# A graph kernel's message pass: one gather per tile of edges instead of one per slot, into a ring of 64 tiles

## What is computed

```python
em = jnp.concatenate([x[src], x[dst]], axis=-1)
em = jax.nn.relu(layer_norm(em @ msg_w + msg_b, msg_g, msg_beta))
em = em * edge_weights[:, None]
msgs = jax.ops.segment_sum(em, dst, num_segments=num_nodes)
```

## Time and profile before

| | us |
|---|---|
| median of 3 runs | 8210.3 (8195.7 to 8234.3) |
| span of the profiled execution | 6732.1 |
| median less that span | 1478.2 |
| first to last gather of the message pass | 4579.7 to 6590.8 |

### The profile page before, as it was taken

The page is one execution under the profiler, slowest core; times in us unless marked ns, Lnnn a source line. Parts: engine busy times, 40 slices in busy tenths (PEclk is TensorE's granted clock), DMA queues, the critical chain, the costliest instruction groups (busy, mean ns, idle before and its releaser), DMA issues. The chain is left out here.

```text
span 6732.1 us, 124645 instructions
## 1 busy us (share of the span) xinstructions
PE 5109.7 (76%) x33726; PEld 4567.4 (68%) x33726; DVE 4555.6 (68%) x15714; ACT 2981.2 (44%) x10333; POOL 4624.6 (69%) x4875
## 2 busy tenths in 40 slices
PE   5788887888887378888888888866676677776775
PEld 4666676676766268777777777856666666666664
DVE  5777777777777746666666665676666666666667
ACT  3444444444444322222222222255666666666666
POOL 4777777777775077777777777706777777777771
PEclk7788888888888656666666676679999999999997
DMA  8544444444443322222222222222222222222221
GB/s 173 151 116 115 115 112 114 115 115 115 114 114 85 103 61 63 64 62 63 63 63 62 64 62 63 62 86 60 54 54 53 54 54 54 54 54 54 54 54 29
DMA packets 334708, 534.90 MB, mean 79 GB/s; under 512 B 105502, under 2 KB 222767, under 8 KB 333665
## 3 DMA queue, kind: packets, MB, share of 16 engines
q0 software_dynamic: 181264, 439.20, 25.7%
q1 hardware_dynamic: 143462, 83.65, 4.6%
q10 hardware_dynamic: 9323, 4.08, 0.3%
HBM read 489.59 MB, written 42.61 MB: 79 GB/s over the span
## 5 line engine op out<-in xcount | busy, mean ns | idle before, releaser
L932 POOL DMA_INDIRECT arena<-rows,slot_src x3222 | 3079.0, 956 | 1027.3 <-issue 930.8
L722 POOL DMA_INDIRECT arena<-msg_rows,slot_src x1611 | 1521.4, 944 | 523.7 <-issue 483.9
L1130 ACT ACTIVATE arena<-psum 128x512 f32<-128x512 bf16 x808 | 480.2, 594 | 1552.3 <-PE psum L978 1528.4
L2034 PE MATMUL psum<-arena 128*128 x3232 | 704.9, 302 | 500.4 <-DMA arena<-msg_rows,slot_src 447.3
L1019 PE MATMUL psum<-arena 128*128 128x145 f32 x3232 | 978.6, 394 | 0.0
L1268 DVE TENSOR_TENSOR arena<-arena,psum 128x290 f32 x1616 | 731.2, 452 | 292.8 <-DVE arena L1268 176.6
L2034 PEld LDWEIGHTS psum<-arena 128*128 128x128 f32 x3232 | 524.6, 204 | 567.6 <-issue 567.4
L1021 PE MATMUL psum<-arena 128*128 128x145 f32 x3232 | 870.1, 360 | 0.0
L2041 ACT ACTIVATE arena<-psum 128x128 bf16<-128x128 f32 x1616 | 424.1, 277 | 754.5 <-PE psum L2036 754.4
L1205 DVE TENSOR_TENSOR arena<-arena,psum 128x512 f32<-128x512 f32 x808 | 553.6, 685 | 262.5 <-PE psum L1021 255.9
L1034 PE MATMUL psum<-arena 128*128 x3232 | 595.9, 326 | 155.9 <-ACT arena L1130 67.3
(11 more groups left out here) (360 smaller groups left out, 9590.5 us busy)
## 6 DMA issues: line engine op xcount, KB each, us to landing
arena<-rows,slot_src POOLq DMA_INDIRECT x3222
arena<-msg_rows,slot_src POOLq DMA_INDIRECT x1611
arena<-slot_keys SPq DMA_DIRECT2D x100, 128.0 KB
edge_alpha<-arena SPq DMA_DIRECT2D x50, 128.0 KB
arena<-edge_alpha SPq DMA_DIRECT2D x50, 128.0 KB
slot_keys<-lane_keys SPq DMA_DIRECT2D x24, 256.0 KB
arena<-rows SPq DMA_DIRECT2D x6, 1024.0 KB, 10.0
rows<-arena SPq DMA_DIRECT2D x4, 822.0 KB
```

Of the source, the lines that this page charges most:

```text
L722: pool.indirect_dma_start(out=self.buffer[:, v % U, j, :], out_offset=None, in_=self.source, in_offset=bass.IndirectOffsetOnAxis(ap=K.SRC[ ...
L932: pool.indirect_dma_start(out=E.rowbuf[:, r, j, :], out_offset=None, in_=E.source, in_offset=bass.IndirectOffsetOnAxis(ap=K.SRC[:, at:at + ...
L1130: act.activation(E.onehotT[:, v % 2, :, :], E.psT, ACT.Copy).then_inc(E.turned, 1)
L2034: pe.matmul(psH[b][:, j, :], onehotT[:, b, j, :], K.by_dst[:, bass.ds(blocks(v, j), 1), :].rearrange("p b w -> p (b w)"), start=True, stop ...
```

## The change

A tile is gathered once. Tile t goes to place t mod 64 of a ring (`RING = 64`), and both slots of a tile that has two read the same place. The gathers are in tile order, so 1563 instead of 1611 are issued. For this the sources must be there by tile: `tile_sources`, new, runs between `attend` and `second_rows`; it loads `src` from DRAM, turns it with PE and stores it as `tile_sources` in DRAM. `node_loads` loads that over `K.SRC` after the second pass has used it. POOL before each gather waits for the visit that last used the place, and for the tile 24 before to have landed (each of 24 semaphores is used by one tile in flight). SP waits for each tile in order and counts one semaphore, `landed`, up. PE waits for `landed` to reach a value that it works out from a block number in a register, and finds the ring place of each slot from a register as well.

```diff
+def message_rows_in(K, source, ring, summed, landed):
+    pool = K.pool
+    for t in range(TILES):
+        last = t - RING + NB - 1
+        if last >= 0:
+            summed.wait(pool, 0, last // G)
+        at_least(pool, landed, t - ROWS_MOST + 1)
+        pool.indirect_dma_start(out=ring[:, t % RING, :], out_offset=None, in_=source,
+                                in_offset=bass.IndirectOffsetOnAxis(ap=K.SRC[:, t:t + 1], axis=0)
+                                ).then_inc(K.arrived[t % ROWS_MOST], 16)
+def message_rows_landed(K, before, landed):
+    sp = K.sp
+    for t in range(TILES):
+        r = t % ROWS_MOST
+        sp.wait_ge(K.arrived[r], before[r] + 16 * (t // ROWS_MOST + 1))
+        sp.sem_inc(landed, 1)
+def tiles_needed(v, block):
+    last = v * G + G - 1
+    return TILES if last >= USED else (last + 1 - block) & 2047
+def tile_place(slot, block):
+    return (slot + RING - block) & (RING - 1)
@@ second_pass
     rstd, mean = attend(K, D)
+    tile_sources(K, D)
     second_rows(K, rstd, mean)
+def tile_sources(K, D):
...
+    converted.done(pool.memset(given_i[:, full // P:SC, :], 0))
+    converted.after(sp)
+    load(sp, moved, given_i[:, 0:full // P, :], D["src"][0:full // P * P * P].rearrange("(c p e) -> p c e", p=P, e=P))
+    load(sp, moved, given_i[0:full % P, full // P, :], D["src"][full // P * P * P:full * P].rearrange("(p e) -> p e", e=P))
...
+    moved.after(pool)
+    converted.done(pool.tensor_copy(given, given_i))
+    converted.after(pe)
+    for half, cs in enumerate((range(0, 8), range(8, SC))):
+        if half:
+            out.after(pe)
+        for c in cs:
+            last = pe.transpose(K.ps[:, 6 + c % 8 // 4, c % 4 * P:c % 4 * P + P], given[:, c, :], K.ident[:, :])
+        flipped.done(last)
+        flipped.after(act)
+        for a in range(cs[0], cs[-1] + 1, 4):
+            n = min(4, cs[-1] + 1 - a)
+            out.done(act.activation(turned[:, a * P:(a + n) * P], K.ps[:, 6 + a % 8 // 4, 0:n * P], ACT.Copy))
+    out.after(sp)
+    load(sp, moved, K.tile_src, turned)
+    moved.after(sp, pool, K.dve, act)
@@ node_loads
         load(sp, S.late[k], S.h1_T[:, a * P:z * P], K.h1_T[:, a * P:z * P])
+    load(sp, S.tiles_in, K.SRC[:, 0:TILES], K.tile_src[:, 0:TILES])
@@ message_pass
+    S.tiles_in.after(pool)
+    pool.wait_ge(S.q_out, len(CHUNKS))
+    message_rows_in(K, K.prow, ring, summed, landed)
+    message_rows_landed(K, arrived_before, landed)
@@ sums
-        gather.emit(i, v)
         ones.out.wait(pe, i, v)
         scaled.wait(pe, i, v - U)
-        gather.arrived.wait(pe, i, v)
+        pe.wait_ge(landed, tiles_needed(v, blocks(v, G - 1)))
...
-            last = pe.matmul(psH[b][:, j, :], K.ident[:, :], rowbuf[:, b, j, :], start=False, stop=True)
+            last = pe.matmul(psH[b][:, j, :], K.ident[:, :],
+                             ring[:, bass.ds(tile_place(v * G + j, blocks(v, j)), 1), :].rearrange("p b w -> p (b w)"),
+                             start=False, stop=True)
```

More of the change, by code:

```diff
@@ L54 @@
 LOADS = [(b, min(b + 4 * CHUNK, NB)) for b in range(0, NB, 4 * CHUNK)]
+RING = 64
 BIG = 1e30
@@ L1590, in attend @@
     return rstd, minus_mean
+TILES_AT = 2 * REGION + (NB + 1) * AW + 2650
+def tile_sources(K, D):
+    pool, pe, act, sp = K.pool, K.pe, K.act, K.sp
+    SW, full = SC * P, E // P
+    given_i, given = K.arena[:, TILES_AT:TILES_AT + SW].bitcast(i32), K.arena[:, TILES_AT + SW:TILES_AT + 2 * SW]
+    given_i, given = (x.rearrange("p (c e) -> p c e", e=P) for x in (given_i, given))
+    turned = K.arena[:, TILES_AT + 2 * SW:TILES_AT + 3 * SW].bitcast(i32)
+    assert TILES_AT + 3 * SW <= ARENA - 1568
+    K.tile_src = K.dram("tile_sources", [P, SW], i32)
+    moved, converted, flipped, out = (K.dmas("tile_sources_moved"), K.relay("tile_sources_converted"),
+                                      K.relay("tile_sources_turned"), K.relay("tile_sources_out"))
+    converted.done(pool.memset(given_i[:, full // P:SC, :], 0))
+    converted.after(sp)
+    load(sp, moved, given_i[:, 0:full // P, :], D["src"][0:full // P * P * P].rearrange("(c p e) -> p c e", p=P, e=P))
+    load(sp, moved, given_i[0:full % P, full // P, :], D["src"][full // P * P * P:full * P].rearrange("(p e) -> p e", e=P))
+    if full * P < E:
+        load(sp, moved, given_i[full % P:full % P + 1, full // P, 0:E - full * P], row_of(D["src"][full * P:E]))
+    moved.after(pool)
[14 more added lines that the diff above has]
+    moved.after(sp, pool, K.dve, act)
 def second_rows(K, rstd, minus_mean):
@@ L1700, in __init__ @@
         self.late = [K.dmas(f"nodes2_late_in{k}") for k in range(len(LOADS))]
+        self.tiles_in = K.dmas("nodes2_tile_sources_in")
 def node_loads(S, D):
@@ L1987, in message_pass @@
     K.acc = table(K.RF, MW)
-    (rowbuf,) = pieces(K.RA, 0, (F, None))
-    onehotW, junk = pieces(K.RA, NB * F, (P, None), (F, bf16))
+    ring = K.RA[:, 0:RING * F].rearrange("p (t w) -> p t w", w=F)
+    onehotW, junk = pieces(K.RA, RING * F, (P, None), (F, bf16))
     onehot, onehotT, rhs = pieces(K.RL, NB * F, (P, bf16), (P, None), (MW, None))
@@ L2002, in message_pass @@
         Event(K, "message_" + x) for x in ("summed", "squared", "rooted", "inverted", "scaled", "ready", "scattered"))
-    gather = Gather(K, "message", K.prow, rowbuf, [summed])
+    landed, arrived_before = K.sem("message_tiles_landed"), list(K.arrived_before)
     ones = OneHots(K, "message", onehot, onehotT, psT, summed, onehotW, scattered)
@@ L2077, in message_pass @@
     for v in (0, 1):
-        sums(0, v, lambda _, j: blocks_pe(v, j))
+        sums(0, v, blocks_pe)
     scales(0, 0, lambda j: None)
@@ L2092, in message_pass @@
             if at + 2 < VISITS:
-                sums(i, v + 2, lambda _, j: blocks_pe(at + 2, j))
+                sums(0, at + 2, blocks_pe)
             ready.wait(pe, i, v)
```

## The result

| | median of the runs | range | span of the profiled execution | its time |
|---|---|---|---|---|
| before, beside the changed kernel | 8221.67 us | 8195.68 to 8234.33 (4) | 6732.1 us | - |
| changed | 8149.23 us | 8134.46 to 8165.84 (4) | 8132.7 us | 8134.46 us |

The ratio is 0.9914, with 0.9895 to 0.9933 as its 95% interval: 0.9% faster, 72 us on these medians. The forecast was 8172 us and -39 us.

A forecast was written before the change was run, and what follows sets the result against it. It took POOL's gathers to bound the message pass. Terms -60.0 + 20.7 + 0.2 + 0.5 = -38.6 us gave a span of 6693.5, plus 1478.2 around it 8172 us (-0.47%); range 8130 to 8240.

The forecast's parts named there:

- What bounds the kernel: Message pass: POOL's gathers, 1.249 us from start to start, set the pace; a visit of four slots costs 4.99 us.
- a rival of 0.10: Time outside the profile: the 1478 us are the same work running slower, so everything scales, 8163 us; chance 0.10.
- The loop's own pace: Message pass: the loop of PE, ACT and DVE takes 4.38 us a visit, below the gathers' new 4.83.
- 48 gathers fewer: Message pass: 48 gathers at 1.249 us each are saved and count in full, -60.0 us.
- PE's registers: Message pass, PE: five more register expressions a visit, 0.23 us, mostly beside matmuls and covered by the gathers; cost 0.
- The bound of a number load: PE's wait on a register's value: at most a load of eight numbers, 1.2 us; taken at the low end.
- the rival of 8567: PE's wait on `landed`: at 1.2 us extra a visit the loop becomes the bound, 336 us more; chance 0.07.
- Waits on POOL and counting by SP: Message pass: POOL's extra waits hide behind the gather before, 0; SP's hop from landing to PE costs 0.2 us once.
- The sources by tile: Between `attend` and `second_rows`: a chain of load, cast, transposes, copies and store, all counted, 20.7 us (bounds 14 and 36).
- Time around the span: Outside the profiled span: 1478.2 us, the median less the span, taken as unchanged.
- slower throughout: Whole kernel: timed work runs 1.22 times slower than profiled, scaling the gain to -47 us, 8163 us; chance 0.10.
- the rival of 8250: Around the span: the surrounding time grows with some 6600 added instructions, 5.3%, +78 us; chance 0.08.

The follow-up runs named there:

- e3: The changed kernel, unedited, timed and profiled against the kernel before on one chip; ratio 0.9949, span 8277.7 us.
- e2: The kernel before, unedited, profiled again on the same chip as the changed kernel; median 8318.76 us, span 8319.5 us.
- e7: Changed kernel with three of four message-pass gathers left out after the first 64; 1777.7 us from first to last scatter.
- e11: Changed kernel with TensorE's ring places and landed wait as constants instead of register values; 2496.7 us from first to last scatter.
- e6: Changed kernel with 49 more gathers in the message pass, into columns nobody reads; 2482.0 us from first to last scatter.
- e4: Kernel before with only the ring of 64 and SyncE's count, one gather per slot, constants on PE, no sources' stretch; ratio to before 1.0021.
- e5: Kernel before with only the sources' stretch added between attend and second_rows, its result unused; ratio to before 1.0038.
- e8: Changed kernel with three of four gathers after the first 64 replaced by memsets of about 0.95 us; 1779.7 us from first to last scatter.
- e10: Changed kernel with the sources' work laid beside attend, transposes behind loop_edges' product; ratio to before 0.9918, 2415.2 us from first to last scatter.

## Why the prediction was right or wrong

The time came out inside the range and on the side that was forecast, but this was in good part luck: the mechanism behind the forecast was not that of the timed runs, and errors in its terms cancelled. By stages e3 against e2 is -77 in the loop, +14 at its start, +12 for the sources and +10 elsewhere, where the forecast had -60, 0, +21 and +1.

**What bounds the kernel: right for the rows shown, wrong for the runs that are timed.** The step that failed is the first, "so the gathers set the pace". At the timed pace POOL is idle for 0.30 us in each of three gaps and for about 1.35 in the fourth, and PE hardly waits for rows (3.9 us in e2, 8.2 in e3). Yet the gathers do set the length of a visit, by a way that the rows ahead of the prediction don't contain: four gathers, then the pause in which PE's signals come through. The hint was in the table: 1478 us between span and median. I priced it as a rival of 0.10 and should have asked first whether the profile was of the runs at all. The loop's own pace, 4.38 us a visit in the prediction, was near: 4.41 in e7.

**48 gathers fewer, -60.0.** From first gather to last scatter the message pass of e3 is 2480.0 us and that of e2 2543.3: -63.3. The size is right by a coincidence of three terms: from first to last gather -116.9, of it 48 x 1.25 = 60 the gathers and 57 what POOL's pauses lost beyond their 0.30; and +53.6 from the last gather to the last scatter (26.3 to 79.9), since at the end POOL runs further ahead and the last visits are done without gathers. By e11 the 60 alone would not have come. With the registers in place, e6 prices a gather at 67 / 49 = 1.37 us, not 1.249.

**PE's registers, 0.** Wrong in kind. They cost 14 us at the start and, with the waits of POOL as they are in this kernel, are a condition of the gain. The 46 ns of the earlier trace rows hold for the one step a slot of before, also in e2 and e11 (1616 of 1616). Of the 9286 steps of e3, 73 took over 0.1 us, mostly 0.7 and at most 1.4, and none of them after the last gather; in e7, with a quarter of the gathers, it is 13, all at the start. The bound of a number load for the wait on a register, and with it the rival of 8567, is refuted.

**Waits on POOL and counting by SP, 0 and 0.2.** Right: the gap inside a group stays 0.30, and "SPq" ended 11.5 us of POOL's idle time in all. e4, which has both, took 6 us more than e2 in the loop, and that comes from its start.

**The sources by tile, 20.7.** The timeline of the changed kernel:

```profile
2861.46 0.46 DVE L1608 RECIPROCAL arena<-arena 128x49 f32<-128x49 f32 x1 [1.37 <-ACT arena L1607]
2861.95 1.43 SPq L184 DMA_DIRECT2D arena<-in_src  x3
2867.18 1.57 POOL L1637 CAST arena<-arena 128x1664 f32<-128x1664 int32 x1 [67.02 <-DMA arena<-in_src]
...
2868.90 1.94 PE L1643 MATMUL psum<-ident,arena 128*128 128x128 f32 x8 [66.55 <-POOL arena L1637]
...
2874.17 0.35 SPq L184 DMA_DIRECT2D tile_sources<-arena  x1
2877.68 2.65 DVE L1672 TENSOR_SCALAR arena<-arena 128x128 f32<-128x128 f32 x10 [15.76 <-DMA tile_sources<-arena]
```

15.8 us. The chain is as predicted and each term a little too dear: load 5.2 (6.0), cast 1.6 (2.3), transposes and copies 5.3 (5.7), store with its hand-over 3.5 (6.0). The formula of the Trainium skill, DMA: Bandwidth & Descriptors (Anatomy of one DMA), which I had weighed and put aside, is stated for transfers that GpSimd issues, and these are SyncE's; as an estimate it gives 3.95 us for the store, nearer to the 3.5 than my row, and 3.8 for the load, where 5.2 were measured. The time between the passes grew by less than DVE's 15.8 us of waiting: 12 us in e3 and in e5. e5, which has the same stretch, was timed at +0.38% (21 to 42 us by its interval), and its span is 22 us longer, of which 6 lie in the loop of the message pass that it leaves as it was; where the rest comes from stays open.

**Time around the span.** The rival "slower throughout" was the true case, and its 8163 the nearest of all the numbers. But it scaled a sum whose parts don't scale: a gather takes 0.94 us at either pace. The time around the span is 1.8 us and did not grow with 10767 instructions more (I had counted 6600), which ends the rival of 8250.

**What is open.** Why one profiled execution of fourteen ran without the hold: it has 1611 gathers 1.249 us apart without a pause, so gathers are needed for the hold but are not enough. What in the chip holds TensorE, and whether it is the issuing or the transfer of the rows. Why the changed kernel's gain was 0.9% in one comparison and 0.5% in the other, where the kernel before took 8222 and 8319 us.

## What to carry to other kernels

Before reading a profile, set its span beside the time of the runs; where they differ by more than a few microseconds, profile once more, since the bound may be another. Where idle time ends in "remote", look at what another engine does up to that moment, and test it by putting other work in its place, as e8 did. In a kernel with gathers from GpSimd, count a visit as its gathers plus a pause, and look at how many gathers are issued in one go: here groups of four went with the shorter loops and groups of eight with the longer ones. A longer lead isn't free, since the gathers ahead have to be issued before anything else goes on (89.2 us for the first visit of e4).

## What the hardware showed that I had not expected

While GpSimd issued gathers of 128 rows without a break, TensorE started one of the two records of an fp32 matmul per 2.8 us in most cases (e4), and its semaphore updates came 1.1 to 1.55 us after the latest gather's end (e3, 1039 of 1143). Memsets of 0.95 us in the gathers' places did nothing of the kind (e8: 4.42 us a visit, against 6.1), and neither did 1611 unbroken gathers in the profile ahead of the prediction. ACT's and DVE's updates are recorded 0.01 us after their instructions' ends (median). And an added cost evened out a loop: with register steps on TensorE the granted clock was 0.93 instead of 0.84, and the loop with the same number of gathers took 81 us less (e11 and e10).
